# Order of an attention loop on PE: three scores ahead of the weighted sum, and the split of the row maxima moved from VectorE to GpSimd

## What is computed

```python
q = (x @ wq).reshape(bsz, toks, NH, HD)       # NH = 32 heads, HD = 16
k = (x @ wk).reshape(bsz, toks, NKV, HD)      # NKV = 8 groups of 4 heads
v = (x @ wv).reshape(bsz, toks, NKV, HD)
scores = jnp.einsum('bqgrd,bkgd->bgrqk', qg, k) / jnp.sqrt(HD)
attn = jax.nn.softmax(scores, axis=-1)
out = jnp.einsum('bgrqk,bkgd->bqgrd', attn, v)
x = layernorm(x + out.reshape(bsz, toks, NH * HD) @ wo)
x = layernorm(x + ffn(x))
```

## Time and profile before

| | us |
|---|---|
| median of 3 runs (866.73, 866.97, 871.05) | 866.97 |
| the profiled execution's own time | 864.86 |
| its span, first to last instruction | 863.1 |
| PE busy in the span | 824.7 |
| DVE busy | 637.7 |
| ACT busy | 390.3 |
| POOL busy | 279.1 |
| mean granted clock of PE, share of full | 0.981 |

### The profile page before, as it was taken

The page is one execution under the profiler, slowest core; times in us unless marked ns, Lnnn a source line. Parts: engine busy times, 40 slices in busy tenths (PEclk is TensorE's granted clock), DMA queues, the critical chain, the costliest instruction groups (busy, mean ns, idle before and its releaser), DMA issues. The chain is left out here.

```text
span 863.1 us, 11538 instructions
## 1 busy us (share of the span) xinstructions
PE 824.7 (96%) x4112; PEld 494.5 (57%) x4112; DVE 637.7 (74%) x868; ACT 390.3 (45%) x721; POOL 279.1 (32%) x324
## 2 busy tenths in 40 slices
PE   6999999999999999999989979999999999999995
PEld 5866433333333333333337657777777777777773
DVE  5578899899999999999208787557955796568554
ACT  4321688687788777878760112222121212112210
POOL 2212235633475355313410623432221121212121
PEclk9999899899999999999998989999999999999998
DMA  7793353233543454333405542310300030002001
GB/s 219 250 285 117 102 111 81 84 108 109 153 141 108 120 152 120 86 97 106 113 25 184 182 140 86 87 60 2 134 13 0 1 122 1 1 0 99 1 1 49
DMA packets 48224, 83.05 MB, mean 96 GB/s; under 512 B 9544, under 2 KB 13640, under 8 KB 48040
## 3 DMA queue, kind: packets, MB, share of 16 engines
q1 hardware_dynamic: 40448, 64.45, 24.4%
q0 software_dynamic: 7440, 16.76, 6.5%
q10 hardware_dynamic: 280, 1.11, 0.4%
HBM read 54.18 MB, written 28.05 MB: 95 GB/s over the span
## 5 line engine op out<-in xcount | busy, mean ns | idle before, releaser
L517 DVE TENSOR_REDUCE neg_max<-ps_pair 128x2 f32<-128x1024 f32 x256 | 303.1, 1216 | 30.1 <-PE ps_pair L632 30.0
L483 ACT ACTIVATE probs<-ps_st 128x512 f32<-128x512 f32 x512 | 267.6, 603 | 72.4 <-PE ps_st L645 72.1
L645 PE MATMUL ps_st<-q,k 50*128 50x512 f32 x512 | 157.5, 478 | 0.5 <-ACT probs L483 0.2
L884 POOL TENSOR_TENSOR g_l<-picked,g_h 128x512 fp32r<-128x512 f32 x56 | 73.1, 1305 | 250.5 <-ACT g_h L934 250.5
L645 PEld LDWEIGHTS ps_st<-q,k 50*128 50x128 f32 x512 | 69.5, 187 | 144.4 <-ACT probs L483 140.4
L659 PE MATMUL ps_pv<-probs,v 128*32 128x512 f32 x1024 | 138.9, 615 | 0.0
L632 PE MATMUL ps_pair<-k,q 48*128 48x512 f32 x512 | 106.6, 449 | 10.0 <-DVE neg_max L517 9.7
L927 ACT ACTIVATE picked<-ps_h 128x512 f32<-128x512 f32 x56 | 33.5, 599 | 181.8 <-PE ps_h L1148 181.8
L991 DVE STREAM_TRANSPOSE turned<-ps_prep 128x512 f32<-128x512 f32 x56 | 40.0, 715 | 93.4 <-PE ps_prep L1123 93.4
L1148 PE MATMUL ps_h<-xt_h,w_h 128*128 128x512 f32 x224 | 87.9, 392 | 0.2 <-ACT picked L927 0.2
L1148 PE MATMUL ps_h<-xt_l,w_h 128*128 128x512 f32 x224 | 87.5, 391 | 0.0
(11 more groups left out here) (141 smaller groups left out, 1153.8 us busy)
## 6 DMA issues: line engine op xcount, KB each, us to landing
operands<-parts POOLq DMA_DIRECT2D x20, 512.0 KB, 4.3
q<-operands SPq DMA_DIRECT2D x64, 128.0 KB, 2.5
sums<-stage SPq DMA_DIRECT2D x32, 256.0 KB, 2.2
x_raw<-xT SPq DMA_DIRECT2D x16, 256.0 KB, 5.1
k<-operands SPq DMA_DIRECT2D x64, 64.0 KB, 2.3
q<-operands SPq DMA_DIRECT2D x64, 64.0 KB, 2.4
att<-sums SPq DMA_DIRECT2D x16, 256.0 KB
yf<-x SPq DMA_DIRECT2D x4, 1024.0 KB, 5.5
```

What stands on the lines that cost most here:

```text
L483: nc.scalar.activation(probs[kt % 2][:, r], ps_st[i % 3][:], ACT.Exp, scale=float(HD) ** -0.5).then_inc(exp_done, 1)
L517: nc.vector.tensor_reduce(neg_max[:, at:at + 2], ps_max[pair % 2][:], AX.X, ALU.max, negate=True).then_inc(max_red, 1)
L645: nc.tensor.matmul(ps_st[i % 3][:], k_[n % QR][64 * a:64 * a + ROWS, kt * P:(kt + 1) * P], q[n % QR][64 * a:64 * a + ROWS, j, :], start=Tr ...
L884: nc.gpsimd.tensor_tensor(g_l[m % 2][:], picked[m % 2][:], g_h[m % 2][:].bitcast(F32), ALU.subtract).then_inc(g_ready, 1)
```

## The change

PE's order within a step becomes r0, r1, two tiles, r2, weigh of the step before, r3, two tiles. Tile 48 no longer goes ahead of the loop. ACT copies a unit's sums out before exponential r3 of the next unit's first step, not before r2. `pairs_at` begins one task earlier, with the V task of batch 1, and gives the last two tasks one pair each. `high_max` and `low_max` become POOL instructions: for unit n + 2 they stand first in POOL's stream for unit n, ahead of load_shift(n + 1). DVE keeps `turn_max`, in the same place.

```diff
-    FIRST_MAXIMA = 2 * TASKS
+    FIRST_MAXIMA = 2 * TASKS - 1
...
         def pairs_at(b, o):
 
-            at = 2 * (TASKS * b + o - FIRST_MAXIMA)
-            return range(max(at, 0), min(at + 2, AHEAD * TILES // 2))
+            task, pairs = TASKS * b + o - FIRST_MAXIMA, AHEAD * TILES // 2
+            twos = pairs - (LAST - FIRST_MAXIMA)
+            if task < twos:
+                return range(max(2 * task, 0), max(2 * task + 2, 0))
+            return range(task + twos, task + twos + 1)
...
+            def high_max(n):
+                at = n % (AHEAD + 1) * TILES
+                src = neg_max[:, at:at + TILES].rearrange("p (t j a) -> p a j t", t=TT, j=2)
+                pool.wait_ge(max_red, TILES // 2 * (n + 1))
+                if n:
+                    pool.wait_ge(max_turned, n)
+                nc.gpsimd.tensor_copy(max_parts[:, :, 0], src).then_inc(max_high, 1)
...
             for n in range(NU):
+                if n + 2 < NU:
+                    high_max(n + 2)
+                    low_max(n + 2)
                 if n + 1 < NU:
                     load_shift(n + 1)
...
-                        if r == 2 and kt == 0 and n:
+                        if r == 3 and kt == 0 and n:
                             take_sums(n - 1)
...
-                        if n + 2 < NU and kt < 2:
-                            (high_max, low_max, turn_max, lambda n: None)[2 * kt + pair % 2](n + 2)
+                        if n + 2 < NU and kt == 1 and pair % 2 == 0:
+                            turn_max(n + 2)
...
-            scores(AHEAD * TILES)
             for n in range(NU):
                 for kt in range(TT):
                     step = n * TT + kt
-                    ahead = 4 * step + AHEAD * TILES + 1
+                    ahead = 4 * step + AHEAD * TILES
                     scores_t(n, kt, 0)
+                    scores_t(n, kt, 1)
                     scores(ahead)
-                    scores_t(n, kt, 1)
+                    scores(ahead + 1)
+                    scores_t(n, kt, 2)
                     if step:
                         weigh(*divmod(step - 1, TT))
-                    scores_t(n, kt, 2)
-                    scores(ahead + 1)
                     scores_t(n, kt, 3)
                     scores(ahead + 2)
                     scores(ahead + 3)
```

More of the change, by code:

```diff
@@ L391, in split_att, with low_max @@
                                         ).then_inc(att_split, 1)
+            def high_max(n):
[5 more added lines that the diff above has]
+                nc.gpsimd.tensor_copy(max_parts[:, :, 0], src).then_inc(max_high, 1)
+            def low_max(n):
+                at = n % (AHEAD + 1) * TILES
+                src = neg_max[:, at:at + TILES].rearrange("p (t j a) -> p a j t", t=TT, j=2)
+                pool.wait_ge(max_high, n + 1)
+                nc.gpsimd.tensor_tensor(max_parts[:, :, 1], src, max_parts[:, :, 0].bitcast(F32),
+                                        ALU.subtract).then_inc(max_split, 1)
             for b in range(NB):
@@ L395, in _ @@
                     store_parts(b, o)
+                    if (b, o) == (2, 3):
+                        high_max(0)
+                        low_max(0)
                     if (b, o) == (2, 4):
@@ L399, in _ @@
                         load_shift(0)
+                        high_max(1)
+                        low_max(1)
                     if (b, o) == (3, 2):
@@ L518, in row_max @@
                                         negate=True).then_inc(max_red, 1)
[L520 to L533, removed]
             def turn_max(n):
@@ L575, in _ @@
                         if TASKS * b + o == FIRST_MAXIMA + 4 * (n + 1):
-                            high_max(n)
-                            low_max(n)
                             turn_max(n)
```

## The result

| | before | after |
|---|---|---|
| median in the comparison, us | 866.85 (4 runs, 860.9 to 871.05) | 851.72 (4 runs, 849.93 to 854.97) |
| ratio, 95% interval | | 0.986 (0.9815 to 0.9905) |
| the profiled execution's own time | 864.86 | 850.92 |
| its span | 863.1 | 848.9 |
| mean granted clock of PE, share of full | 0.981 | 0.989 |

The change makes the kernel 1.4% faster. The forecast was 854.8, in the range 849.5 to 863.5.

What follows compares the result with a forecast made beforehand. A ring of PE and ACT, neither full, bounds the loop at 2.67 us a step. -8.0 + 3.1 - 4.9 - 2.2 - 0.2 = -12.2 takes 864.86 to 852.7; with 2.1 for the median, 854.8, range 849.5 to 863.5.

Steps and rivals of the forecast that it cites:

- The order: PE's loop steps: one exponential, not two, between weighs; 2.60 instead of 2.67 us over 115 steps, 8.0 us less.
- the first rival: Ahead of weigh, the score's drain takes 0.49, so the order gains nothing; 862.8 us, chance 0.20.
- The last 12 steps: Loop's end, PE itself the bound: three scores need a further row-group turn, 11 x 0.29 less 0.1, 3.1 us more.
- The split: Maxima split leaves DVE, so stalls of its cast behind long POOL instructions go; 4.9 us less.
- The low clock near 165: PE's clock at 0.51 after the longest stall; without that stall it should not fall, 2.2 us less.
- The low clock at the loop's start: A like low-clock stretch just after the loop's start, left as it is; no gain counted.
- POOL's price: Split on POOL: 0.2 per instruction plus 0.1 for semaphores, 0.5 us in all, hidden by 3.8 us of cover.
- The 875 by that rule: Skill's elementwise rule: 0.68 on the path of 30 units, about 20 us above forecast; at most chance 0.05.
- The second rival: At turn_max, POOL becomes DVE's bound; up to about 0.8 us late is free; 881 at 1.7 late, chance 0.05.
- The load of the maxima: load_shift, behind the wait in POOL's stream, issued some 1 us into a unit, needed in the next: costs nothing.
- The third rival: In each loop step, row groups do not hide the third score, adding about 0.34; step 2.94, 894 us, chance 0.04.
- The start: Loop's start: one pair in each of the last tasks removes tile 48's wait for DVE; 0.2 us less (0 to 1.5).

Runs made afterwards that it cites:

- 12 copies: Changed kernel, POOL writing the high parts 12 more times ahead of each unit's split from unit 2 on; 866.39 us (one run).
- the four pieces: Changed kernel with each reciprocal of the denominators cut into four pieces of 32 columns, one behind each of four row maxima; 848.97 us (one run).
- 20 copies: Changed kernel, POOL writing the high parts 20 more times ahead of each unit's split from unit 2 on; 934.01 us (one run).
- the run again: Changed kernel unaltered, measured once more in the second comparison; 851.42 us (4 runs), ratio 0.9838 to the kernel before.
- the version with even steps: Changed kernel; last 12 steps with third score behind weigh, sums copied at the old place; reciprocal in four pieces; 846.88 us (4 runs), ratio 0.9789.

## Why the prediction was right

The forecast of the likeliest case was 852.7 for the profiled execution; it took 850.92, and the median 851.72 stands against 854.8. Step by step:

- **The order, 8.0 less.** Right in mechanism: r2 is loaded 0.05 after r3's exponential and weigh follows 0.43 later (0.42 taken, 0.49 was the first rival's). In size the term is 7.0: I took 0.07 per step from 2.67 and 2.60, and the whole units give 0.245 per four steps, 0.061 each. The order alone, in its own kernel, has the same steps, so the first rival is out.
- **The last 12 steps, 3.1 more.** Right in mechanism, 2.45 in size. The further turn of a row group costs 0.25 (0.67 - 0.42), not the 0.29 of a project_out matmul. The shorter last interval is as taken (2.56 to 2.66). Putting r2 back returned 2.0 in these intervals and 0.4 in the one ahead of them.
- **The split, 4.9 less.** As forecast: no long step is left but the three reciprocals, and the split alone removes them under the old order too. What stood behind it, DVE's cast held by POOL's long instruction, came back in the kernel with the order alone (2.49 beside 4.01). The Trainium skill says in GPSIMD Engine Reference, section Specifications, that GpSimd's SBUF interfaces are shared with VectorE, with contention for DVE instructions in a 2-port mode or with two SBUF inputs. The trace before agrees on the subtraction, which has two such inputs: it once took 1.14 (229.78 to 230.92) and ended 0.03 after POOL's 1.27 from 229.62. The cast has one and was held as well; in what mode it ran no trace shows. The row maxima, which read PSUM, kept their 1.22, and 12 or 20 short copies of POOL did not stretch DVE's transposes beyond 0.21.
- **The low clock near 165, 2.2 less.** It went. In the kernel with the order alone the stall stayed, and so did a low stretch right behind it; with 12 copies a longer stall brought a longer one. That PE was "mostly idle" in the stall was read too strongly: its records cover 2.91 of the 4.11 us from 160.76.
- **The low clock at the loop's start.** I had left it as it was; it was gone, another 2.2, and that is the largest miss. Its cause is open. It differs from one execution to the next, but not by chance alone as far as the record goes. The eight traces with the new order have none seven times and 3.4 us once (the four pieces); the two with the old order have 6.8 and 13.7. In the 5 us ahead of the loop's first weigh PE is busy for 3.68 in the kernel before (88 to 93) and 3.91 in the split alone, where it waits twice for DVE (0.52 and 0.65 before, 0.52 and 0.46 there), but for 4.52 or 4.53 in all eight traces with the new order. Of ten runs of the split alone, nine have a mean clock of 0.982 to 0.985; of eight runs of the changed kernel, seven have 0.987 to 0.992. So the 2.2 may well belong to the order or to the new places of the first pairs; no run changed the loop's start by itself. Two of the 19 runs of the kernel before in the first comparison have 0.989, as much as the changed kernel's trace, which has no low clock in its loop; so it seems that in the kernel before too neither stretch is always there.
- **POOL's price, 0.5 behind 3.8 of cover.** 0.51 was measured (166.59 to 167.11 in the worst unit), and 0.36 us of the cover remained there, where 0.5 was forecast. In a clean unit the cover was 3.6 (split from 174.42, transpose at 178.01). The elementwise rule of GPSIMD Engine Reference in the Trainium skill, section Engine selection, about two times slower with two inputs, is not borne out at this size: 0.22 against DVE's 0.17. Even doubled, it would have stayed under the cover. The 875 by that rule did not come, because the price is off the path.
- **The second rival's free 0.8.** Measured 0.54 to 0.68. Its mechanism is real: past that every bit of lateness is paid, and with 20 copies the kernel is 68 us slower than before. The change is faster because POOL is on time, by 0.36 us in one unit and by 3.1 in a clean one. The load of the maxima, called "nothing", costs nothing only while that holds.
- **The third rival**, a step of 2.94, is out: r2 behind the tiles costs nothing in the loop, since those run beside r3's exponential. Its price of 0.34 had no row; where a third score does cost, in the last steps, it is 0.25.
- **The start, 0.2 less.** The loop began 0.6 earlier in this trace, but 0.7 later in the run again (93.78 against 93.05), so no gain is shown.
- **The sum.** The forecast was 12.2 less, and the spans differ by 14.2. The order gave 1.0 less than forecast and the last steps cost 0.65 less; that these two misses offset each other is luck. The stretch at the loop's start (2.2), 0.4 more at the start and the reciprocals (0.3) were not in the sum, and the part behind the loop took 0.4 more.

## What to carry to other kernels

In a ring between two engines, count which instructions stand between one release and the next, and move out those that need no release. Here one exponential of two left the ring, and the gain was less than that, since the moved score then had to leave the array first. The same order cost time in the stage where PE itself is the bound, so such an order should be chosen by stage. Here the small work went better to the engine that had slack in time than to the one that does it fastest. But read the slack at the worst unit: at 3.1 us of slack in a clean unit and 0.36 in the worst, 3.2 us more work cost nothing in the first and 10 us in the other.

## What the runs showed of the hardware

- A small DVE instruction that reads SBUF was held until a long POOL instruction ended: a cast of 0.17 took 2.49 and ended at 158.63, POOL's at 158.60. Row maxima, which read PSUM, were not.
- A stall of PE can be paid twice. In the kernel with the order alone a step of 4.28 was followed by 3.4 us at clock 0.50 and a step of 3.80 instead of 2.6; with 12 copies the clock fell during a wait of 7.32, and steps of 4.07 and 3.77 followed. It is not always so: behind a step of 3.91 one unit earlier, and behind three of 3.50 to 3.73 with 12 copies, the steps are 2.6 and 2.7 again.
- At the loop's start the granted clock was low for 0, 3.4, 6.8 or 13.7 us, which moves single runs by up to 4 us (three steps of 4.06, 4.07 and 3.83 where 2.67 each is due). The kernel before spread over 10 us in 19 runs, the version with even steps over 1.3 in four; how much of that is the clock was not tried.
- Three scores in two row groups take 0.67, two take 0.42 to 0.43: the third costs 0.25, less than a further pair.
